# Zero fillers in bf16 from the start, the first steps of phase 1 in another order, and four loads on ScalarE's queue

## What is computed

```
x = x + linear_attention(layernorm(x))      # 16 heads of 8; feature map exp(proj - 0.5*|.|^2)
x = x + slot_block(layernorm(x))
# linear_attention, per sequence and head:
q, k, v = rows @ Wq.T + bq, rows @ Wk.T + bk, rows @ Wv.T + bv
q', k'  = feature_map(q, R), feature_map(k, R)
kv = sum_n k'_n v_n^T ; z = 1 / sum(q') ; out = (q' kv) z @ Wo.T + bo
# slot_block:
o = slots + mha(slots, x, x; d_W*, d_b*)    # 16 slots per sequence read from the 256 rows
o = o + expert_ffn(layernorm(o))            # one expert per slot, 128 -> 512 -> 128, gated
out = mha(x, o, o; c_W*, c_b*)              # the 256 rows read from the 16 slots
```

## Time and profile before

| what | value |
|---|---|
| median of three runs | 185.29 us (184.99 to 185.3) |
| span of the profiled execution | 184.4 us |
| PE busy | 175.9 us, 95% of the span |
| DVE, ACT, POOL busy | 137.0, 119.0 and 139.6 us |
| share of PE in the chain that ended last | 85% |
| granted TensorE clock, mean | 1.000 |

### The profile page before, as it was taken

One profiled execution on the slowest core, in us unless ns is written; L12 is line 12 of the kernel. 1 busy time (PEld: TensorE's weight loads), 2 busy tenths in 40 slices (PEclk: granted clock), 3 DMA queues, 4 the chain that ended last, 5 costly groups with the idle time before them and its releaser, 6 DMA issues.

```text
span 184.4 us, 4825 instructions
## 1 busy us (share of the span) xinstructions
PE 175.9 (95%) x1512; PEld 133.2 (72%) x1512; DVE 137.0 (74%) x398; ACT 119.0 (65%) x296; POOL 139.6 (76%) x276
## 2 busy tenths in 40 slices
PE   6989999999999999999999999899999999999994
PEld 5935777778877787788778877423676589989993
DVE  3728888798878859585889578666537996979891
ACT  2226457779779777768676777338415787756881
POOL 4675597989789987969976668315958768798893
PEclk9999999999999999999999999999999999999999
DMA  4719996999999410000000000000000001121123
GB/s 126 237 27 308 381 299 153 376 325 375 315 379 219 142 38 2 0 4 4 0 4 0 0 5 0 5 0 0 4 0 0 4 0 34 57 87 52 38 82 119
DMA packets 20955, 19.35 MB, mean 105 GB/s; under 512 B 1433, under 2 KB 16354, under 8 KB 20930
## 3 DMA queue, kind: packets, MB, share of 16 engines
q1 hardware_dynamic: 20066, 18.39, 32.1%
q10 hardware_dynamic: 864, 0.66, 1.1%
HBM read 16.95 MB, written 2.10 MB: 103 GB/s over the span
## 4 chain that ended last, share of the span: by engine, by line
PE 85%; DVE 6%; ACT 3%; issue 2%; DMA 1%; SPq 1%; POOL 0%; DVEq 0%
PE ps L1243 16%; PE ps L1318 8%; PE ps L1559 8%; PE ps L1499 6%; PE ps L1253 5%; PE ps L1276 4%; PE ps L1299 4%; PE ps L1356 4%; PE ps L1531 4%; PE ps L1266 3%; PE ps L1310 2%; PE ps L1522 2%; PE ps L1289 2%; PE ps L1430 2%; PE ps L1449 2%
## 5 line engine op out<-in xcount | busy, mean ns | idle before, releaser
L1243 PE MATMUL ps<-Wproj,xnT 128*128 128x512 f32 x64 | 31.6, 617 | 0.8 <-ACT xnT L631 0.8
L925 DVE TENSOR_REDUCE ss<-sq 128x64 f32<-128x512 f32 x16 | 10.9, 683 | 13.3 <-ACT sq L607 13.3
L531 POOL TENSOR_TENSOR Wgs<-Wgs,W2s 128x256 f32<-128x256 f32 x30 | 17.8, 622 | 1.7 <-DVE W2s L1111 1.5
L1243 PEld LDWEIGHTS ps<-Wproj,xnT 128*128 128x128 f32 x64 | 11.4, 199 | 9.5 <-issue 8.2
L1318 PE MATMUL ps<-XN2T,Ad 128*128 128x256 f32 x64 | 16.7, 384 | 0.0
L600 ACT ACTIVATE pr<-ps,nmax 128x256 f32<-128x256 f32 x32 | 14.9, 473 | 2.0 <-DVE nmax L964 1.7
L1559 PE MATMUL ps<-W1s,W2s 128*128 128x128 f32 x120 | 15.9, 278 | 0.0
L1559 PEld LDWEIGHTS ps<-W1s,W2s 128*128 128x128 f32 x120 | 14.6, 191 | 0.7 <-ACT W2s L749 0.4
L540 POOL TENSOR_TENSOR W2s<-W2s,X 128x256 f32<-128x256 f32 x15 | 11.0, 743 | 5.2 <-PE ps L1531 3.2
L460 POOL TENSOR_SCALAR xn<-X,nm,rs 128x127 f32<-128x127 f32 x30 | 14.0, 476 | 1.2
L607 ACT ACTIVATE sq<-ps 128x512 f32<-128x512 f32 x16 | 9.6, 599 | 8.2 <-PE ps L1243 8.2
(11 more groups left out here) (207 smaller groups left out, 503.5 us busy)
## 6 DMA issues: line engine op xcount, KB each, us to landing
W1s<-in_L_ffn_e_W_dram SPq DMA_DIRECT2D x4, 1024.0 KB, 8.2
Wgs<-in_L_ffn_e_Wg_dram SPq DMA_DIRECT2D x4, 1024.0 KB, 8.4
W2s<-in_L_ffn_e_W_dram SPq DMA_DIRECT2D x16, 256.0 KB, 8.3
out_dram<-W2s SPq DMA_DIRECT2D x15, 128.0 KB, 1.7
X<-in_L_attn_x_dram SPq DMA_DIRECT2D x3, 512.0 KB, 7.1
hbias<-in_L_ffn_e_bg_dram SPq DMA_DIRECT2D x8, 64.0 KB, 2.1
X<-in_L_attn_x_dram ACTq DMA_DIRECT2D x2, 128.0 KB, 2.5
X<-in_L_attn_x_dram ACTq DMA_DIRECT2D x1, 256.0 KB, 3.0
```

Source lines behind the costliest of these rows:

```text
L531: last = pool.tensor_tensor(heads(at[:, k, j * HS:(j + 1) * HS], S), heads(ep[:, k, j * HS:(j + 1) * HS], S), over(rsm[:, k, j * H:(j + 1) ...
L1243: last = pe.matmul(banks(b)[:, j, :], xnT[:, k, j * P:(j + 1) * P], Wproj[:, :], start=True, stop=True)
```

## The change

Four things are changed in the order of work; the remaining lines of the diff turn loops into named steps and move a wait into the step that needs it.

1. `warm(n)` multiplies a 128x128 tile `fill` of bf16 zeros by itself. DVE clears that tile as its first instruction (`set_fill`). The counts become 28, 2, 2 and 4.
2. On PE, `project(1)` is split into its two halves, and `turn_xn(2)` stands between them. On POOL, `other_masks` goes behind `apply1(3)`.
3. The four blocks of 16 slot rows are loaded by ACT's queue, behind `keep_xnT(0)`. They still count to `w_slots`.
4. The two broadcast biases `d_bo` and `c_bo` go behind `w_rest` in SP's list, with a semaphore `bo_in` of their own; `slots_residual` (DVE) and the first `out_bias` (POOL) wait for it.

The diff, cut to its core:

```diff
+        fill = sb("fill", P, P, dtype=BF16)
...
-        N_SLOTS, N_REST = 17, 4
+        N_SLOTS, N_REST, N_BIASES = 15, 4, 2
...
             load(sp, w_slots, (a_bo_all[:, :], a_bo.partition_broadcast(P)), (W[:, DK, :], d_Wk),
-                 (W[:, DV, :], d_Wv), (W[:, CQ, :], c_Wq), (W[:, DQ, :], d_Wq),
-                 (vec[SLOT:SLOT + S, :], slot.rearrange("o s d -> (o s) d")), (vec[GAIN:GAIN + S, :], ln_g),
-                 (vec[SHIFT:SHIFT + S, :], ln_b), (vec[B2:B2 + S, :], b2), row(BDK, d_bk), row(BDV, d_bv),
-                 row(BCQ, c_bq), row(BDQ, d_bq), row(BCK, c_bk), row(BCV, c_bv),
-                 (d_bo_all[:, :], d_bo.partition_broadcast(P)), (c_bo_all[:, :], c_bo.partition_broadcast(P)))
+                 (W[:, DV, :], d_Wv), (W[:, CQ, :], c_Wq), (W[:, DQ, :], d_Wq), row(BDK, d_bk), row(BDV, d_bv),
+                 row(BCQ, c_bq), row(BDQ, d_bq), row(BCK, c_bk), row(BCV, c_bv))
...
             load(sp, w_rest, (W[:, DO, :], d_Wo), (W[:, CK, :], c_Wk), (W[:, CV, :], c_Wv), (W[:, CO, :], c_Wo))
+            load(sp, bo_in, (d_bo_all[:, :], d_bo.partition_broadcast(P)), (c_bo_all[:, :], c_bo.partition_broadcast(P)))
...
-            rstd1(0); rstd1(1); apply1(1); rstd1(3); apply1(2); other_masks(); apply1(3); rstd1(5)
+            rstd1(0); rstd1(1); apply1(1); rstd1(3); apply1(2); apply1(3); other_masks(); rstd1(5)
...
+            def load_slot_rows():
+                load(sc, w_slots, (vec[SLOT:SLOT + S, :], slot.rearrange("o s d -> (o s) d")),
+                     (vec[GAIN:GAIN + S, :], ln_g), (vec[SHIFT:SHIFT + S, :], ln_b), (vec[B2:B2 + S, :], b2))
+
-            keep_weights(); keep_feature_weights(); keep_xnT(0); squares(0); keep_xnT(1); keep_value_weights()
+            keep_weights(); keep_feature_weights(); keep_xnT(0); load_slot_rows(); squares(0); keep_xnT(1); keep_value_weights()
...
-            sc.wait_ge(h_in, 16 * 3 * EG)
...
+            def set_fill():
+                ve.memset(fill[:, :], 0.0).then_inc(fill_ok, 1)
+
-            repeat_identity(); stats1(0); moments1(0); center_weights(); set_biases(); spread_rotation(); apply_first(); stats1(1)
+            set_fill(); repeat_identity(); stats1(0); moments1(0); center_weights(); set_biases(); spread_rotation(); apply_first(); stats1(1)
...
             def warm(n):
-                pe.wait_ge(ident_ok, 1)
+                pe.wait_ge(fill_ok, 1)
                 for _ in range(n):
-                    pe.matmul(ps[:, 2, 0:P], ident[:, :], ident[:, :], start=True, stop=True)
+                    pe.matmul(ps[:, 2, 0:P], fill[:, :], fill[:, :], start=True, stop=True)
...
-            warm(5); turn_biases(); repeat_rotation(); warm(2); turn_weights(); warm(1); feature_weights(); turn_xn(0); warm(2)
-            project(0); turn_xn(1); turn_value_weights(); project(1); turn_xn(2); key_sums(0); project(2)
+            warm(28); turn_biases(); repeat_rotation(); warm(2); turn_weights(); warm(2); feature_weights(); turn_xn(0)
+            warm(4); project(0); turn_xn(1); turn_value_weights(); project_half(1, 0); turn_xn(2)
+            project_half(1, 1); key_sums(0); project(2)
```

More of the change, by code:

```diff
@@ L227, in build @@
         w_slots, w_rest, e_in, slots_in, slots_set = (sem(n) for n in ("w_slots", "w_rest", "e_in", "slots_in", "slots_set"))
-        h_in, bias_set = sem("h_in"), sem("bias_set")
+        h_in, bias_set, bo_in = sem("h_in"), sem("bias_set"), sem("bo_in")
         f_in, parts_act, parts_pool = sem("f_in"), sem("parts_act"), sem("parts_pool")
@@ L462, in apply2, with out_bias @@
                 last.then_inc(xn2_ok, 1)
[L464 to L471, removed]
-            rstd1(0); rstd1(1); apply1(1); rstd1(3); apply1(2); other_masks(); apply1(3); rstd1(5)
+            def out_bias(b):
+                if b == NB - 1:
+                    pool.wait_ge(xn2_last, 1)
+                else:
+                    pool.wait_ge(xn2_ok, b + 1)
+                if b == 0:
+                    pool.wait_ge(bo_in, 16 * N_BIASES)
+                pool.tensor_tensor(rows(b), rows(b), under(c_bo_all[:, :], 2), ALU.add).then_inc(xcbo_ok, 1)
+            rstd1(0); rstd1(1); apply1(1); rstd1(3); apply1(2); apply1(3); other_masks(); rstd1(5)
             scale_features(0); add_bias(0); slot_rows(); scale_features(1); add_bias(1); rstd2(0); apply2(0)
@@ L485, in _, with clear_hT, slot_rstd @@
             rstd2(14); apply2(14); rstd2(15)
[L487 to L491, removed]
+            def clear_hT():
+                wait(pool, mbp_ok, NB)
+                pool.memset(hT[:, :, :], 0.0).then_inc(hT_zero, 1)
+            def slot_rstd(n):
+                groups = slice(*UNITS[n])
                 pool.wait_ge(mv3_ok, n + 1)
@@ L495, in _, with products @@
                 pool.tensor_tensor(rs3[:, groups], ve3[:, groups], mhalf[:, groups], ALU.pow).then_inc(rs3_ok, 1)
-            for g in range(G - 1):
+            def products(g):
                 pool.wait_ge(sg_ok, 2 * g + 2)
@@ L501, in _ @@
                 pool.tensor_tensor(act[:, g % 2], sg[g % 2][:, 0, :], sg[g % 2][:, 1, :], ALU.mult).then_inc(act_ok, 1)
-            out_bias(8, NB)
+            clear_hT()
+            out_bias(0); out_bias(1); out_bias(2); out_bias(3); out_bias(4); out_bias(5); out_bias(6); out_bias(7)
+            slot_rstd(0); slot_rstd(1); slot_rstd(2); products(0); products(1); products(2)
+            out_bias(8); out_bias(9); out_bias(10); out_bias(11); out_bias(12); out_bias(13); out_bias(14); out_bias(15)
             def spread_keys(b):
@@ L849, in slots_residual @@
                 ve.wait_ge(slots_in, 16 * EG)
+                ve.wait_ge(bo_in, 16 * N_BIASES)
                 ve.wait_ge(ex_ok, NB)
@@ L1076, in first_keys @@
             def first_keys():
+                ve.wait_ge(xcbo_ok, NB)
                 ve.wait_ge(scaled_ok, 1)
@@ L1234, in slot_sums, with project_half @@
                 last.then_inc(rzp_ok, 1)
-            def project(b):
[L1237 to L1244, removed]
+            def project_half(b, j):
+                k = b % 2
+                if j == 0:
+                    if b == 0:
+                        pe.wait_ge(su_act, 1)
+                    wait(pe, xnT_ok, b + 1)
+                    wait(pe, ex_ok, BANKS_FREE[b])
+                half = pe.matmul(banks(b)[:, j, :], xnT[:, k, j * P:(j + 1) * P], Wproj[:, :], start=True, stop=True)
+                if j == 1:
+                    half.then_inc(proj_ok, 1)
+            def project(b):
+                project_half(b, 0)
+                project_half(b, 1)
             def attention_out(b):
@@ L1396, in _, with slot_projection @@
             turn_pr(15); slot_sums(3); queries(2); slots(15); slot_sums(4); queries(3)
[L1398 to L1401, removed]
+            def slot_projection(half):
+                if half == 0:
+                    pe.wait_ge(ao_ok, len(POST))
+                    pe.wait_ge(w_rest, 16 * N_REST)
+                    pe.wait_ge(slots_set, 2)
                 for g in (2 * half, 2 * half + 1):
@@ L1406, in _, with warm3 @@
                 last.then_inc(o_ok, 1)
-            for _ in range(1):
+            def warm3():
                 pe.matmul(ps[:, BANK_TURN, 0:P], ident[:, :], ident[:, :], start=True, stop=True)
@@ L1412, in hidden_bias @@
                 i = 2 * g + u
+                if i == 0:
+                    pe.wait_ge(parts_act, 3)
+                    pe.wait_ge(rep3_ok, 1)
+                    wait(pe, q2_ok, QUERIES2)
                 wait(pe, sg_ok, i - 3)
@@ L1425, in experts_in @@
             def experts_in(g, u):
+                if (g, u) == (0, 0):
+                    pe.wait_ge(e_in, 16 * (8 + S))
                 pe.wait_ge(hT_ok, min(g + 1, len(UNITS)))
@@ L1473, in slot_values_out @@
                 pe.matmul(ps[:, BANK_V, cols], W[:, CV, :], o2T[:, cols], start=True, stop=True).then_inc(kvp_ok, 1)
[L1475 to L1480, removed]
+            slot_projection(0); slot_projection(1); warm3()
+            hidden_bias(0, 0); hidden_bias(0, 1); hidden_bias(1, 0); turn_xh(0); hidden_bias(1, 1)
             experts_in(0, 0); turn_xh(1); experts_in(0, 1); experts_in(1, 0); turn_xh(2); experts_in(1, 1)
```

11 lines of the change are left out of this document (7 added, 4 removed).

## The result

| | before | after |
|---|---|---|
| median of 20 runs each | 185.28 us (184.94 to 185.92) | 184.06 us (183.68 to 185.74) |
| ratio after / before | | 0.9939, 95% interval 0.9923 to 0.9955 |
| span of the profiled execution | 184.4 | 183.9 |
| its own time | not recorded | 185.69 |

The change makes the kernel 1.2 us faster, a little under half of the 2.5 that were forecast; the time lies inside the range. The profiled execution of after is one of its slowest: of 38 executions of after in all series, 33 had a span of 182.7 or less and three, this one among them, 183.9 or more.

The account below looks back on a forecast made before the run. PE, busy 95% of the span, was taken as the bound. Cheaper fillers and an earlier clock, less the rearrangement's 0.2 to 0.8, start `project(2)` 2.1 to 2.7 earlier, taken as 2.5: 185.3 - 2.5 = 182.8, range 182.3 to 184.7.

Parts of the forecast that it names:

- The fillers' price: PE's start: 28 bf16 fillers at 0.107 each, 1.05 to 4.05, end before the bias load lands at 4.20, costing nothing.
- the fillers do more than they say: Rival: at 0.21 each the first 28 fillers end at 7.0 and delay `turn_biases`; 185.1, no change; chance 0.06.
- The other fillers shrink: PE's setup behind `turn_biases`: f32 fillers of 1.15 + 0.43 + 0.85 become 0.8 at most, partly in waits.
- The steps of the setup with an early clock: PE's setup, clock high from about 5 us: `project(0)` starts at 6.75 and ends 3.4 earlier than 11.87.
- `squares(0)` right behind `project(0)`: ACT: the four load issues, 1.7, lie under `project(0)`, so `squares(0)` loses 0 to 0.1.
- The split: PE's `project(1)`: `turn_xn(2)` between its halves, transposes 0.22 and a wait for POOL, costs 0.2 to 0.8.
- The baseline: Whole kernel: span 184.4 and median 185.29, so 0.9 lies around the span and stays; 185.3 - 2.5 = 182.8.
- The same distance from project(2) to the end: From `project(2)` to the end: nothing changes, so what its start gains, the kernel gains.
- behind it all five lists are unchanged: Ground for carrying the gain at `project(2)` to the end; the moved waits there were put at nothing.
- The clock rises later, though before its old moment: Rival, PE's setup: rise at 9 gives 183.6, at 11.2 gives 184.6; range 183.2 to 184.7, chance 0.24.
- The clock rises later than before: Rival: clock low through `project(1)`, `project(2)` up to 1.0 later; 185.7 to 186.4, chance 0.12.
- the list of signs to watch: Profile signs, including filler times and `project(2)` at 13.05 to 13.65; double-length records up to 11 us would refute the forecast.

Follow-up runs that it names:

- unsplit: After with `project(1)` whole again and `turn_xn(2)` behind it; 183.83 us, ratio to before 0.9919.
- after_again: After run once more without any edit; 184.25 us, ratio to before 0.9922.
- dense: After with 3 fillers added behind `turn_biases`, 3 instead of 2 behind `repeat_rotation`, 8 instead of 4 ahead of `project(0)`; 184.36 us, ratio to before 0.9965.
- after_third: After run another time without any edit, in a later series; 183.95 us, ratio to before 0.9926.
- lean: Before plus the bf16 fillers and moved loads, with PE's and POOL's order and the other waits as before; ratio to before 0.9906, repeated 0.9923.
- before_again: Before run once more without any edit; 185.75 us, ratio to before 0.9996.
- fill_only: Before with only the new bf16 fillers and the clearing of their tile; 184.52 us, ratio to before 0.9961.
- no_fill: After without any fillers; 185.77 us, ratio to before 1.0025.
- f32_fill: After with the old f32 identity fillers, counts 5, 2, 1 and 2; 185.84 us, ratio to before 1.0017.
- lean_first: `lean` with only the first 28 fillers, the 2, 2 and 4 left out; 185.47 us, ratio to before 0.9974.

## Why the prediction was half right

**The fillers' price: right.** The forecast was a start at 1.05, one every 0.107, and an end at 4.05. Measured: 1.04 and 3.17 for 28 with the last one's tail, `turn_biases` at 4.22 against 4.33 in the earlier trace rows. The rival "the fillers do more than they say" is out.

**"The other fillers shrink": right, with a smaller saving.** 2.43 of f32 fillers were to become 0.8 at most. At the low level they measured 1.35 and 0.33, so 1.0 was saved where 1.6 stood.

**The steps of the setup with an early clock: right to 0.2 to 0.4.** `project(0)` was put at 6.75 and stands at 6.94 in `unsplit`; `project(1)` at 9.45 and stands at 9.85. `project(2)` was put at 13.05 to 13.65 and stands at 13.67 in `after_again`, 13.14 in `dense`, 12.80 in `unsplit`. With a late clock `project(0)` was put at 7.6, and 7.81 and 7.84 were measured. `squares(0)` right behind `project(0)` is as said. The split costs 0.22 to 0.36 where 0.2 to 0.8 stood.

**The baseline: wrong, and the larger part of the miss.** The step that failed is "The span is 184.4 and the median of the runs 185.29, 0.9 around it, which the change leaves". The gain was worked out against a trace whose clock rose at 11.0 and then taken off a median of runs in most of which it rose earlier. The term put at 0.9 measured 1.76 to 1.95, by the medians of the series of before, so the trace was 184.4 - 183.5 = 0.9 longer than the median execution. Taken off the trace, -2.5 forecasts a span of 181.9; after's median is 182.35. Taken off the median, it counts 0.9 that the old fillers already had in most runs. The prediction knew the reason: the Trainium skill (TensorE: Matmul & The Clock Gate, Part 1) says that the moment of the rise varies between runs of one kernel. The traces here agree: 8.4 and 11.0 in before, 6.8, 9.7 (`after_third`) and 10.2 in after. But the sentence was applied to after alone, and the three runs within 0.31 were read as speaking against a scatter. They said only that three draws came out alike; 20 runs of after spread over 2.06.

**"The same distance from project(2) to the end": mis-sized by 0.2 to 1.0.** The change of this distance was put at nothing, on the ground that "behind it all five lists are unchanged", although waits were moved there; it measured 0.23, 0.47 and 0.99 in the three traces of after. I took PE's steps behind `project(2)` in `before` and in the traces of after and compared their shifts, in us:

| step | `after` | `after_again` | `after_third` | `lean` |
|---|---|---|---|---|
| `project(2)` | -0.69 | -2.09 | -0.90 | -2.57 |
| last `project` | -0.81 | -2.21 | -1.02 | -2.70 |
| slot output projection | -0.62 | -2.04 | -0.85 | -2.53 |
| first expert products | -0.53 | -1.95 | -0.76 | -2.54 |
| second expert products | -0.47 | -1.89 | -0.69 | -2.54 |
| end of the last product | -0.47 | -1.88 | -0.68 | -2.55 |
| end of the span | -0.46 | -1.62 | +0.09 | -2.33 |

The first loss, 0.17 to 0.19, is a wait of DVE on its own result ahead of the slot output projection. DVE's timeline there, of `before_again` and then of `fill_only`:

```profile
114.48 0.23 DVE L884 TENSOR_TENSOR pvm<-ps,head 128x64 f32<-128x64 f32 x1 [0.16 <-PE ps L1266]
114.74 0.26 DVE L890 TENSOR_REDUCE pvs<-pvm 128x16 f32<-128x64 f32 x1
```

```profile
113.16 0.23 DVE L885 TENSOR_TENSOR pvm<-ps,head 128x64 f32<-128x64 f32 x1 [0.16 <-PE ps L1270]
113.60 0.26 DVE L891 TENSOR_REDUCE pvs<-pvm 128x16 f32<-128x64 f32 x1 [0.21 <-DVE pvm L885]
```

The 0.21 ahead of the second step stands in every trace in which DVE clears the fill tile first, even in `no_fill`, and in neither trace of before. Why it does is open: the tile and its semaphore are new in the same kernels, and no run took the clear alone away. The next two losses, 0.09 and 0.06, come at the first and second expert products, in after, `f32_fill`, `no_fill` and `unsplit`, and not in `lean` or `fill_only`: they belong to the other order or the moved waits, which the prediction put at nothing. PE's timeline at the first of them, `before_again` and `after_again`:

```profile
119.00 1.07 PE L1430 MATMUL ps<-W1s,qz 128*32 128x512 f32 x8 [0.43 <-DVE qz L1042]
```

```profile
118.25 1.06 PE L1459 MATMUL ps<-W1s,qz 128*32 128x512 f32 x8 [0.52 <-DVE qz L1058]
```

The last loss comes behind the last product: 0.26 in `after_again`, 0.77 in `after_third`, 0.22 in `lean`, nothing in `after`. So it isn't the change as such. SP's queue at the end, `after`, `after_again` and `after_third`:

```profile
177.47 4.07 SPq L339 DMA_DIRECT2D out_dram<-W2s  x5
```

```profile
176.06 4.43 SPq L339 DMA_DIRECT2D out_dram<-W2s  x5
```

```profile
177.25 5.07 SPq L339 DMA_DIRECT2D out_dram<-W2s  x5
```

Five stores took 0.36 and 1.00 longer to issue than in `after`, and the last store stands behind them. In `lean` the last store is issued in time (2.56 earlier than in before) and the span ends 0.22 later behind it. Why the stores differ so is open; they add to the scatter of the spans beside the clock.

**The sum.** Forecast -2.5; 0.9 of it was in the baseline; some 0.2 to 0.5 goes behind `project(2)` (1.0 in `after_third`). That leaves 1.1 to 1.4, and 1.15 to 1.2 was measured. The two terms are shown by runs and traces. That they close the sum takes the 2.5 at `project(2)` as met in the median execution, and this is an estimate: the traces of after show 0.69, 0.90 and 2.09, at spans of 183.9, 184.5 and 182.8, and none lies at the median of 182.35. With 184.4 - 182.35 = 2.05 and a loss of 0.2 to 0.5 behind it, `project(2)` would start 2.3 to 2.6 earlier there.

**The rivals.** "The clock rises later, though before its old moment" (184.6 where it stays at 11.2) is what the profiled execution of after shows, with a rise at 10.2; spans of 183.9 or more are the exception there, 3 of 38. "The clock rises later than before" showed in no median. What the list of signs to watch said holds: records of double length up to 10.2 in `after`, and the time of that execution, 185.69, is 1.63 above the median.

**What is left open.** Why the moment of the rise wanders; whether and why bf16 fillers bring it forward where f32 ones do less, for which there are eight traces against three; and whether `dense` had more late executions than after, since 3 of 11 against 3 of 38 can be chance. No version beat after for certain: `lean` (0.9906, then 0.9923) and `unsplit` (0.9919) lie within its interval.

## What to carry to other kernels

A profile is one execution: set its span only against the time of that same execution, and where a stage depends on something that wanders between runs, have more than one trace of before, or work from both its ends, before taking a difference from it. Products that fill a wait at the start can pay through TensorE's clock although nobody reads them, if they are cheap: here the early clock saved 1.57 in the first projection, and the small fillers cost 1.35 in f32 and 0.33 in bf16. Count executions by when the clock rose, not one trace. When a stage moves forward, look at what it now meets first: here a semaphore shared by 17 loads, harmless in the old trace, made PE wait 0.94.

## What the hardware showed that was not expected

- The moment at which TensorE went from its low to its high level lay between 3.84 us (`dense`) and 10.97 us (before), in `lean_first` later still, and 3.4 us apart in two executions of one kernel (`after_again` and `after`). It moves `project(2)` by some 2 us of a span of 184: it starts at 12.80 in `unsplit` (rise at 5.11) and at 15.07 in `after` (10.18), 0.22 of it for the split.
- The granted clock in the page read full in every slice while records took twice their time, in `after` as in the earlier trace rows. The trace's record of the clock begins only with the rise, and the page takes what lies before as full. The durations of equal records agree with that first entry: 11.0 and 10.2 by them, 10.97 and 10.18 by the record.
- The time around the span was 1.7 to 2.4 us in before, 1.7 to 2.7 in `f32_fill`, and 1.7 to 1.8 in after.
- One added instruction at the head of DVE's list, with its tile and semaphore, went with a wait of 0.21 us of DVE on its own result 113 us later, in all 12 traces that have it and in neither of before. That the instruction is the cause is not shown.
